# Four of the first key head's five projections, with their rotations, moved beside the last head of the full attention; the causal stage's later projections at other steps

## The chip, the cores and the metric

The kernel runs on one core of one Trainium2 chip. Its time is the device time of one launch, in microseconds (us): the median of three runs was 2612.7 us (2612.5 to 2613.82). TensorE (PE), VectorE (DVE), ScalarE (ACT) and GpSimd (POOL) run their own instruction streams in program order and meet at semaphores; SyncE (SP) issues the large transfers.

## The reference, cut to what matters

Two layers of a small model, each an attention-like part and a mixture of experts, on x of shape (2, 1024, 256). The change lies in the second layer: a full attention of three heads, a norm, and a causal attention with rotary embedding, 16 query heads in 4 groups that share a key head.

```python
# full attention, per batch b (0, 1) and head h (0, 1, 2)
scores = Q @ K.T / sqrt(256); w = softmax(scores over the queries' axis); attn = w @ V
x = x + ga * (mean(attn over the heads) @ fc_w.T + fc_b)
...
# causal attention, HD 128, per batch and key head (4), each with 4 query heads
q = x @ wq; k = x @ wk; v = x @ wv
apply_rope(x) = concat([x1 * cos - x2 * sin, x2 * cos + x1 * sin])
probs = softmax(causal(q @ k.T / sqrt(HD))); out = (probs @ v) @ wo
```

## The kernel before

The program is a chain of stages with a barrier between them: modulation, a state-space layer, the first experts, `attn1` (full attention), `attn2` (causal attention), the second experts. Every stage is written as a list `todo` that each engine's loop walks through in the same order, taking what is its own; so the list alone sets the order on each engine.

A float32 product is made of three passes: each operand is split into a high half (ACT copies it) and a low half (POOL or DVE subtracts), and PE multiplies high by high, high by low and low by high.

`attn1` has 2 batches x 3 heads x 8 rows of scores. One row: PE makes a score unit of 12 matmuls (L1545) into two banks of the accumulator memory; DVE takes the maximum (L1704); ACT makes the exponential (L1605) and its high half (L1610); POOL makes the low half (L1726); DVE makes the scaled values (L1682 to L1689); two rows later PE adds the row's `sum` of 24 matmuls (L1559). Score, key, value and flip (transpose) units share two pairs of banks in turn, so `unit_free` makes each unit wait until the unit two before it has been read: a score by the exponential, a key by its low half on DVE (L1701). DVE also does one piece of a list of `chores` after each row's maximum: in batch 1 those are the residual, the norm and the scaling for the causal stage. The two flips that make `hT` for `attn2` stand behind the last head's rows 6 and 7 and wait for the scaled rows (L1312).

`attn2` has 8 groups u (batch and key head), each with rows 7 to 0 of scores for four query heads. A group needs five projections (`project`, i = 0 the key, 1 to 4 the queries; PE L2143, 12 matmuls each). Each is rotated: DVE multiplies by cos and by sin from the accumulator (L1986 to L1988, called a rotation below), POOL adds the two products (`add`, L2009), ACT copies the high half (`high`, L2059), and the low half is subtracted on DVE for the key (L1992) and on POOL for the queries (`low`, L2014). Two pairs of buffers hold the products, so a query's rotation waits for the low half of the projection two before it:

```python
if i >= 3:
    dve.wait_ge(s["rope"], heads(u, i - 2))
elif i == 2:
    dve.wait_ge(s["rope_k"], u + 1)
```

For group 0 all five projections stand at the stage's start, followed by the four scores of row 7, the values unit and the first `turn`. For u > 0 they stand inside the previous group's rows 4 to 2, between `turn` (four transposes of the probabilities, L2178), `value` (L2188) and `out` (the row's output product, L2197). `turn` and `out` share two banks in turn (`ring_free`): a turn that comes two after an out waits until DVE has added that output to `hs` (L2002). While group 0 runs, DVE also works through 30 chores, one per turn (residual, statistics, norm).

Of the kernel before, what the change touches and what calls it, by code (L numbers as in the profile page):

```python
# [1328 lines left out]
class Ahead:  # L1329


    def __init__(self, ctx, nc, g, hs):
# [3 lines left out]
        self.hT, self.wh = ([sb(n + half, shape, F32R) for half in ("hi", "lo")] for n, shape in (("hT", [P, KC, L]), ("wh", [P, KC, WC])))  # L1336
        self.mask, self.ident_b = sb("mask", [P, P], BF16), sb("ident_b", [P, P], BF16)
# [35 lines left out]
def attn1(nc, g, pre, fc_w, fc_b, norm_w, wq, wk, wv):  # L1373
# [7 lines left out]
    with ctx:  # L1381
# [8 lines left out]
        wm = [sb("wm" + half, [P, 2 * AH, KC, D], F32R) for half in ("hi", "lo")]  # L1390
        late_hT = [sb("hT" + half, [P, KC, L], F32R) for half in ("hi", "lo")]
        fw, fbw = hs[:, TB:TB + KC, :], hs[:, TB + KC, :]
        kT = [sb("kT" + half, [P, 2, KC, L], F32R) for half in ("hi", "lo")]
# [11 lines left out]
        s_nb, s_e, s_eh, s_el, s_vs, s_av, s_acc = sem("nb"), sem("e"), sem("eh"), sem("el"), sem("vs"), sem("av"), sem("acc")  # L1405
        s_next, s_nh, s_nl, s_bf = sem("next"), sem("nh"), sem("nl"), sem("bf")
# [6 lines left out]
        def rows_of(b):  # L1413

            return hs[:, 0:TB, :] if b == 0 else hs[:, TB:2 * TB, :]

        PROJ = ("key", "key", "val", "val")

        def order():
# [34 lines left out]
        units = [t for t in todo if t[0] in ("flip", "key", "val", "score")]  # L1454
# [23 lines left out]
        def _(pe):  # L1478
# [16 lines left out]
            def unit_free(n):  # L1495

                if n >= 2:
                    t = units[n - 2]
                    if t[0] == "score":
                        pe.wait_ge(s_e, row[t[1:]] + 1)  # L1500
                    elif t[0] == "val":
                        pe.wait_ge(s_v, kept[t])
                    else:
                        pe.wait_ge(s_lo, split[t])

            for t in todo:
                what, b, h, i = t
                if what in ("flip", "key", "val", "score"):
# [3 lines left out]
                if what == "flip":  # L1512
# [4 lines left out]
                    tr.then_inc(s_unit, 1)  # L1517
                elif what == "key":
# [20 lines left out]
                elif what == "score":  # L1539
                    if i == 0:  # L1540
                        pe.wait_ge(s_lo, split["key", b, h, 1])
                    for c in range(2):
                        for k in range(KC):
                            for x_, y_ in THREE:
                                mm = pe.matmul(ps[:, o + c, :], kT[x_][:, (b * AH + h) % 2, k, i * P:(i + 1) * P], hT_of(b)[y_][:, k, c * 512:(c + 1) * 512],  # L1545
# [18 lines left out]
        def _(act):  # L1564
# [19 lines left out]
            roots = {(0, 0, 3): (1, 2), (1, 1, 1): (0, 3), (1, 2, 2): (0, 4)}  # L1584
            for t in todo:
# [4 lines left out]
                elif what == "key":  # L1590
                    act.wait_ge(s_unit, number[t] + 1)
                    act.activation(kT[HI][:, (b * AH + h) % 2, i, :], pair(number[t]), ACT.Copy).then_inc(s_hi, 1)
# [5 lines left out]
                elif what == "score":  # L1598
# [11 lines left out]
                    act.activation(eh[HI][:, r % RING, :], e[:, r % 2, :], ACT.Copy).then_inc(s_eh, 1)  # L1610
# [682 lines left out]
```

## Time and profile before

| what | us |
|---|---|
| median of three runs | 2612.7 |
| the profiled execution | 2608.71 |
| its span in the trace | 2606.8 |
| start of `attn1`'s first flip | 993.91 |
| end of `attn1` and start of `attn2` on PE | 1353.44 |
| first turn of `attn2` | 1410.43 |
| end of `attn2`, about | 2296.03 |

PE is busy for 2358.8 us, 90% of the span, DVE for 54%, ACT and POOL for 43% each. The profile is one execution. Its times are from the start of the span; "idle before" of a row names the engine and line that ended the wait. A matmul's busy time overlaps that of the next, so the pace is read from start to start.

### The profile page before, as it was taken

The numbers are of one execution on the slowest core, as the hardware profiler recorded it, in microseconds if no ns is written. First come the engines' busy times: TensorE is split into PE (matmuls) and PEld (weight loads), VectorE is DVE, ScalarE is ACT, GpSimd is POOL, SyncE is SP. The second block draws the span as 40 slices with busy tenths as digits, with TensorE's granted clock in tenths as the row PEclk, the third lists the DMA queues.
The fourth block names the chain that finished last, engine by engine and source line by source line (L and its number), as shares of the span: only waits on it lengthen the run. The fifth ranks groups of instructions, "written<-read, shape, count | busy, mean of one in ns | idle before, by whom it ended". The sixth has DMA issues, their size and how long they took to land. (4 is left out here: it accounts for less than half of the span.)

```text
span 2606.8 us, 34398 instructions
## 1 busy us (share of the span) xinstructions
PE 2358.8 (90%) x12718; PEld 1789.0 (69%) x12718; DVE 1400.7 (54%) x2467; ACT 1119.6 (43%) x1906; POOL 1125.9 (43%) x656
## 2 busy tenths in 40 slices
PE   6959999986999968999986999999999999949997
PEld 2339999964777746899974676777677677725554
DVE  6568888864222225545555855556455554463332
ACT  3467777721111114344433554545455454521121
POOL 0439999901332212443335455444545544203443
PEclk8979999997999988999998999999999999979999
DMA  6273271238211220000000000000000001045223
GB/s 242 94 306 69 75 306 70 102 101 271 49 31 32 34 77 32 1 1 1 1 21 33 21 1 21 21 1 21 1 21 3 18 9 33 1 151 160 44 44 63
DMA packets 109334, 168.33 MB, mean 65 GB/s; under 512 B 30546, under 2 KB 78674, under 8 KB 107092
## 3 DMA queue, kind: packets, MB, share of 16 engines
q1 hardware_dynamic: 94196, 145.35, 15.9%
q0 software_dynamic: 14976, 20.78, 4.8%
q8 instruction: 107, 1.75, 0.3%
q14 instruction: 55, 0.45, 0.1%
HBM read 115.94 MB, written 52.32 MB: 65 GB/s over the span
## 5 line engine op out<-in xcount | busy, mean ns | idle before, releaser
L638 POOL TENSOR_TENSOR mb_dbx<-mb_ud,mb_bb 128x1024 f32<-128x1024 f32 x128 | 302.0, 2364 | 56.2 <-DVE mb_h L496 40.7
L496 DVE TENSOR_TENSOR_SCAN mb_h<-ps,mb_dbx 128x1024 f32<-128x1024 f32 x128 | 292.2, 2288 | 47.9 <-ACT ps L608 37.4
L2025 POOL TENSOR_TENSOR a_e<-a_e,a_rc 128x1024 f32<-128x1024 f32 (+5 forms) x144 | 188.5, 1315 | 269.5 <-DVE a_rc L1945 269.2
L2188 PE MATMUL ps<-a_eT,a_v 128*128 128x512 f32 x576 | 297.4, 598 | 4.3 <-ACT a_eT L2069 4.3
L1955 DVE TENSOR_REDUCE a_mx<-ps 128x1 f32<-128x1024 f32 (+7 forms) x256 | 192.7, 753 | 196.1 <-PE ps L2167 195.4
L939 POOL DMA_INDIRECT e_acc<-e_hid,e_ids x78 | 123.7, 1586 | 370.8 <-DVE e_hid L1235 363.0
L2069 ACT ACTIVATE a_eT<-ps 128x512 f32<-128x512 f32 x288 | 171.1, 594 | 247.5 <-PE ps L2178 246.9
L740 PE MATMUL ps<-mb_dg,mb_hts 128*128 128x128 f32 x2048 | 250.7, 276 | 0.4
L740 PEld LDWEIGHTS ps<-mb_dg,mb_hts 128*128 128x128 f32 x2048 | 239.5, 192 | 1.9 <-issue 1.9
L2164 PE MATMUL ps<-a_kThi,a_qThi 128*128 128x512 f32 (+3 forms) x384 | 205.4, 535 | 22.7 <-DVE a_e L1988 11.0
L1221 DVE COPY e_work<-ps 128x256 f32<-128x256 f32 x78 | 33.2, 425 | 356.7 <-PE ps L1054 356.7
L1726 POOL TENSOR_TENSOR a_elo<-a_e,a_ehi 128x1024 fp32r<-128x1024 f32 x48 | 115.2, 2400 | 231.8 <-ACT a_ehi L1610 121.0
L2053 ACT ACTIVATE a_e<-ps,a_nb 128x1024 f32<-128x1024 f32 (+5 forms) x192 | 156.3, 814 | 91.9 <-DVE a_nb L1956 79.1
L1085 PE MATMUL ps<-e_wd,e_work 128*128 (+1 forms) x780 | 189.0, 384 | 1.9 <-ACT e_work L984 1.9
L1066 PE MATMUL ps<-e_wg,e_work 128*128 x468 | 178.2, 518 | 4.7 <-DVE e_work L1221 1.3
L978 ACT ACTIVATE e_hid<-ps 128x688 f32<-128x688 f32 (+1 forms) x78 | 52.5, 673 | 300.2 <-PE ps L1066 300.2
L617 ACT ACTIVATE mb_hts<-ps 128x512 f32<-128x512 f32 x256 | 139.2, 595 | 93.2 <-PE ps L725 93.2
L1066 PE MATMUL ps<-e_wu,e_work 128*128 x468 | 170.9, 501 | 0.0
L2178 PE MATMUL ps<-ident,a_e 128*128 128x128 f32 x992 | 150.3, 274 | 18.5 <-DVE hs L2002 16.2
L725 PE MATMUL ps<-ident,mb_h 128*128 128x128 f32 x1024 | 135.4, 276 | 32.6 <-DVE mb_h L496 32.4
L1085 PEld LDWEIGHTS ps<-e_wd,e_work 128*128 128x128 f32 (+1 forms) x780 | 138.9, 190 | 30.0 <-issue 15.8
L925 POOL DMA_INDIRECT e_xin<-e_rows,e_ids x78 | 77.2, 990 | 188.3 <-DVE e_ids L1210 164.5
(345 smaller groups left out, 5331.3 us busy)
## 6 DMA issues: line engine op xcount, KB each, us to landing
mb_bb<-mb_db_rows SPq DMA_DIRECT2D x16, 1024.0 KB, 12.2
mb_ddiag<-mb_dg SPq DMA_DIRECT2D x1, 8192.0 KB, 22.3
mb_dg<-mb_ddiag SPq DMA_DIRECT2D x8, 1024.0 KB, 13.3
e_wg<-in_g SPq DMA_DIRECT2D x8, 688.0 KB, 10.3
e_wu<-in_u SPq DMA_DIRECT2D x8, 688.0 KB, 10.5
e_wd<-in_d SPq DMA_DIRECT2D x8, 640.0 KB, 11.1
mb_dxa<-mb_bb SPq DMA_DIRECT2D x8, 512.0 KB, 2.6
mb_dz<-mb_xz SPq DMA_DIRECT2D x8, 512.0 KB, 2.9
```

Of the source, the lines that this page charges most:

```text
L496: dve.tensor_tensor_scan(h[:, at % 2, :], pair(at % 2), dbx[:, at % 2, :], 0.0, ALU.mult, ALU.add).then_inc(s_h, 1)
L638: pool.tensor_tensor(dbx[:, at % 2, :], ud[:, kk % 2, 0, :], bb[:, n, :], ALU.mult).then_inc(s_dbx, 1)
L740: mm = pe.matmul(ps[:, 6 + half, q * P:(q + 1) * P], hts[:, at % 2, c:c + P], dg[:, n, c:c + P], start=(n == 0 and q == 0), stop=(n == NS ...
L1066: mm = pe.matmul(ps[:, b0 + a, 0:FN], xT[:, i % 2, k * P:(k + 1) * P], w[:, ds(e), k, a * FN:(a + 1) * FN].rearrange("p a n -> p (a n)"), ...
L1085: mm = pe.matmul(ps[:, 6, 0:D], hT[0:n, i % 2, c * P:(c + 1) * P], wd[0:n, ds(e), c, :].rearrange("p a n -> p (a n)"), start=(c == 0), sto ...
L1955: own(dve.reduce_max(mx[:, q:q + 1], pair(n, (i + 1) * P), AX_X))
L2025: pool.tensor_tensor(probs(i, h), probs(i, h), rc[:, q:q + 1].to_broadcast([P, (i + 1) * P]), ALU.mult).then_inc(s["en"], 1)
L2053: act.activation(probs(i, h), pair(n, (i + 1) * P), ACT.Exp, bias=nb[:, q:q + 1], scale=SCALE, accum_out=sm[:, q:q + 1]).then_inc(s["e"], 1)
L2069: act.activation(eT[:, k % ER, :], ps[:, bank[what, u, i, h], :], ACT.Copy).then_inc(s["eT"], 1)
L2164: mm = pe.matmul(ps[:, o + t, 0:c1 - c0], qT[x_][:, j, i * P:(i + 1) * P], kT[y_][:, c0:c1], start=(x_ == y_), stop=(x_ == LO and not last))
L2178: tr = pe.transpose(ps[:, bank[token], h * P:(h + 1) * P], probs(i, h, j * P, (j + 1) * P), ident[:, :])
L2188: mm = pe.matmul(ps[:, 6 + rows[u, i] % 2, :], v[:, j, :], eT[:, k % ER, :], start=(j == 0), stop=(j == i))
```

## The change

Group 0's projections 0 to 3 (`AHEAD = 4`) go into `attn1`'s list as `rope` units, after rows 0, 2, 4 and 6 of the last head. Their rotations use one pair of product buffers (`turned`), so rotation i + 1 waits for the low half of projection i. To have `hT` ready, the two flips move one head earlier and DVE does two chores per row instead of one in batch 1 (the list got empty places so that the square roots on ACT still come in time). The results live in buffers that `attn1` no longer needs then. `attn2` starts with projection 4 alone. For u > 0 the projections stand at other turns, and the high halves follow one step later. The number of projections, rotations, adds, and halves is the same as before, except that the key's low half of group 0 is made on POOL instead of DVE.

```diff
+        AHEAD = pre.AHEAD
+        turned = [hs[:, TB + 4 * a:TB + 4 * a + 4, :].rearrange("p a d -> p (a d)") for a in range(2)]
...
-                        if h + 1 == AH and b + 1 == B and m >= 6:
+                        if (b, h) == (B - 1, AH - 2) and m >= 6:
                             todo.append(("flip", B, 0, m - 6))
+                        if (b, h) == (B - 1, AH - 1) and m % 2 == 0 and m // 2 < AHEAD:
+                            todo.append(("rope", B, 0, m // 2))
...
+                    elif t[0] == "rope":
+                        pe.wait_ge(s_rot, t[3] + 1)
...
+                elif what == "rope":
+                    if i == 0:
+                        pe.wait_ge(s_lo, split["flip", B, 0, 1])
+                        pe.wait_ge(s_nl, WPIECES)
+                    c0 = (REP if i == 0 else i - 1) * HD
+                    for c in range(2):
+                        for k in range(KC):
+                            for x_, y_ in THREE:
+                                mm = pe.matmul(ps[:, o + c, :], pre.wh[x_][:, k, c0:c0 + HD], pre.hT[y_][:, k, c * 512:(c + 1) * 512],
...
-            roots = {(0, 0, 3): (1, 2), (1, 1, 1): (0, 3), (1, 2, 2): (0, 4)}
+            roots = {(0, 0, 3): (1, 2), (1, 0, 5): (0, 3), (1, 1, 3): (0, 4)}
...
+                    if ropes:
+                        rope_high(ropes.pop(0))
...
-                    if chores[b]:
-                        chores[b].pop(0)()
+                    for _ in range(1 if b == 0 or (h, i) == (0, 0) else 2):
+                        if chores[b]:
+                            chores[b].pop(0)()
+                elif what == "rope":
+                    o, (a, c) = number[t], turned
+                    if i > 0:
+                        dve.wait_ge(s_roped, i)
+                    else:
+                        dve.wait_ge(s_hi, split["flip", B, 0, 1])
+                    dve.wait_ge(s_unit, o + 1)
+                    dve.tensor_tensor(a, pair(o), pre.cos, ALU.mult)
...
+                if what == "rope":
+                    pool.wait_ge(s_rot, i + 1)
+                    pool.tensor_tensor(turned[0], turned[0], turned[1], ALU.add).then_inc(s_turned, 1)
+                    ropes.append(i)
...
+                    if ropes:
+                        rope_low(ropes.pop(0))
...
-            ahead_proj = {(4, 0): 0, (4, 2): 1, (4, 4): 2, (3, 2): 3, (2, 1): 4}
-            for n in range(NPROJ):
+            ahead_proj = {(4, 0): 0, (4, 1): 1, (4, 3): 2, (3, 0): 3, (3, 3): 4}
+            for n in range(AHEAD, NPROJ):
                 put("project", 0, n, 0)
...
-                while unhigh and (unhigh[0][2] >= 3 or len(unhigh) > 2):
+                while unhigh and (unhigh[0][2] >= (3 if unhigh[0][0] == 0 else 4) or len(unhigh) > 2):
```

Three places in the built programs show what moved. First POOL at the end of `attn1` and the start of `attn2` (`a_elo` is a row's low half, `h_qklo` and `h_wmlo` are the low halves of the projections). Before, then after:

```order
L1726 TENSOR_TENSOR a_elo<-a_e,a_ehi 128x1024 x16
L1381 UNCONDITIONAL_BRANCH
L2004 UNCONDITIONAL_BRANCH
L2009 TENSOR_TENSOR a_e<-a_e 128x1024 x3
L2014 TENSOR_TENSOR a_qTlo<-a_e,a_qThi 128x1024
L2009 TENSOR_TENSOR a_e<-a_e 128x1024
L2014 TENSOR_TENSOR a_qTlo<-a_e,a_qThi 128x1024
L2009 TENSOR_TENSOR a_e<-a_e 128x1024
L2014 TENSOR_TENSOR a_qTlo<-a_e,a_qThi 128x1024 x2
```

```order
L1780 TENSOR_TENSOR hs<-hs 128x1024
L1787 TENSOR_TENSOR a_elo<-a_e,a_ehi 128x1024
L1774 TENSOR_TENSOR h_wmlo<-hs,h_wmhi 128x1024
L1787 TENSOR_TENSOR a_elo<-a_e,a_ehi 128x1024
L1780 TENSOR_TENSOR hs<-hs 128x1024
L1787 TENSOR_TENSOR a_elo<-a_e,a_ehi 128x1024
L1774 TENSOR_TENSOR h_wmlo<-hs,h_wmhi 128x1024
L1385 UNCONDITIONAL_BRANCH
L2069 UNCONDITIONAL_BRANCH
L2074 TENSOR_TENSOR a_e<-a_e 128x1024
L2079 TENSOR_TENSOR h_wmlo<-a_e,h_wmhi 128x1024
```

The adds and low halves now alternate with the rows' low halves in `attn1`, and one of each is left at the start of `attn2`.

Second PE near the output of row 4 (`a_wo`), in the rows before group 1 begins. The first transposes (`ident`) behind the output are free to go; the second ones wait for that output's add on DVE. Before, then after:

```order
L2143 MATMUL ps<-h_hThi,h_whlo 128x512
L2178 MATMUL ps<-ident,a_side 128x128 x4
L2197 MATMUL ps<-a_wo,a_ao 128x256 x4
L2188 MATMUL ps<-a_eT,a_v 128x512
L2178 MATMUL ps<-ident,a_side 128x128 x4
L2188 MATMUL ps<-a_eT,a_v 128x512
L2178 MATMUL ps<-ident,a_e 128x128 x4
```

```order
L2245 MATMUL ps<-ident,a_side 128x128 x4
L2264 MATMUL ps<-a_wo,a_ao 128x256 x4
L2255 MATMUL ps<-a_eT,a_v 128x512
L2208 MATMUL ps<-h_hThi,h_whhi 128x512
...
L2208 MATMUL ps<-h_hThi,h_whlo 128x512
L2245 MATMUL ps<-ident,a_side 128x128 x4
L2255 MATMUL ps<-a_eT,a_v 128x512
L2245 MATMUL ps<-ident,a_e 128x128 x4
```

Projection 3, which ended just ahead of the output's turn, now stands two turns earlier, and projection 4 comes between the output and the turn that waits for its add.

Third DVE while group 0's rows 4 and 3 run, from the end of one rotation (that of projection 2 before, of projection 3 after) over a chore of statistics (`n_st` to `n_var`) to the add of row 4's output (`hs<-ps,hs`). Before, then after:

```order
L1988 TENSOR_TENSOR x<-ps,raw 64x1024
L1269 BN_STATS n_st<-hs 128x6 x4
L1276 TENSOR_TENSOR n_mean<-n_st 128x8
...
L1285 TENSOR_SCALAR n_var<-n_var 128x8
L1986 TENSOR_TENSOR x<-ps,raw 128x1024
L1987 TENSOR_TENSOR x<-ps,raw 64x1024
L1988 TENSOR_TENSOR x<-ps,raw 64x1024
L2002 TENSOR_TENSOR hs<-ps,hs 128x256
```

```order
L2053 TENSOR_TENSOR x<-ps,raw 64x1024
L1269 BN_STATS n_st<-hs 128x6 x2
L1276 TENSOR_TENSOR n_mean<-n_st 128x8
...
L1285 TENSOR_SCALAR n_var<-n_var 128x8
L2067 TENSOR_TENSOR hs<-ps,hs 128x256
L2051 TENSOR_TENSOR x<-ps,raw 128x1024
```

The statistics stood ahead of the fourth rotation and now stand behind it, directly ahead of the output's add.

## Rows read from the trace of the kernel before

**Rows 1.** Busy time by stretch: us, then busy of PE, PEld, DVE, ACT, POOL, PEclk, DMA.

```profile
1353.40:1410.40 57.00, 33.00 (x143) 24.91 (x144) 27.48 (x32) 12.97 (x18) 27.90 (x12) 0.82 0.08 24
...
1472.20:1508.10 35.90, 31.54 (x143) 22.33 (x142) 34.79 (x42) 13.94 (x21) 15.78 (x6) 1.00 0.00 0
```

**Rows 2.** PE's waits, 1320 to 2296 us: us in total, times, longest.

```profile
PE ps L2178 <- DVE hs L2002: 16.2, 8, 3.5
PE ps L2164 <- DVE a_e L1988: 11.0, 2, 5.5
PE ps L2164 <- POOL a_qTlo L2014: 6.2, 1, 6.2
PE ps L1516 <- DVE hs L1312: 3.6, 1, 3.6
```

**Rows 3.** PE in order of time, start of the causal stage: start, us.

```profile
1353.44 0.47 PE L2143 MATMUL ps<-h_hThi,h_whhi 128*128 128x512 f32 x1 [0.32 <-PEq L1381]
...
1400.35 0.23 PE L2167 MATMUL ps<-h_mask,h_ident_b 128*128 128x128 bf16 x1
...
1410.43 0.63 PE L2178 MATMUL ps<-ident,a_e 128*128 128x128 f32 x4 [2.32 <-DVE a_e L1948]
```

**Rows 4.** DVE, POOL and ACT there, in order of time.

```profile
1382.40 1.23 DVE L1986 TENSOR_TENSOR a_e<-ps,raw 128x1024 f32<-128x1024 f32 x1 [4.85 <-POOL a_qTlo L2014]
...
1386.13 1.23 DVE L1955 TENSOR_REDUCE a_mx<-ps 128x1 f32<-128x1024 f32 x1
...
1377.63 2.37 POOL L2009 TENSOR_TENSOR a_e<-a_e 128x1024 f32<-128x1024 f32 x1 [3.88 <-DVE a_e L1988]
1379.95 2.35 POOL L2014 TENSOR_TENSOR a_qTlo<-a_e,a_qThi 128x1024 fp32r<-128x1024 f32 x1
...
1387.58 1.12 ACT L2053 ACTIVATE a_e<-ps,a_nb 128x1024 f32<-128x1024 f32 x1 [15.05 <-DVE a_nb L1956]
...
1391.80 1.99 ACT L2059 ACTIVATE a_qThi<-a_e 128x1024 fp32r<-128x1024 f32 x2
```

**Rows 5.** PE in the full attention's last head, in order of time.

```profile
1322.86 0.40 PE L1545 MATMUL ps<-a_hThi,a_kThi 128*128 128x512 f32 x1
...
1325.60 0.28 PE L1559 MATMUL ps<-a_vhi,a_ehi 128*128 128x256 f32 x1
...
1328.48 0.40 PE L1545 MATMUL ps<-a_hThi,a_kThi 128*128 128x512 f32 x1
```

**Rows 6.** POOL, DVE and PE where the first two keys are split.

```profile
1193.99 2.41 POOL L1726 TENSOR_TENSOR a_elo<-a_e,a_ehi 128x1024 fp32r<-128x1024 f32 x1 [5.27 <-PE ps L1559]
...
1258.49 2.39 POOL L1726 TENSOR_TENSOR a_elo<-a_e,a_ehi 128x1024 fp32r<-128x1024 f32 x1 [5.95 <-PE ps L1559]
...
1194.58 2.37 DVE L1654 TENSOR_TENSOR hs<-hs,mod 128x512 f32<-128x512 f32 x1 [4.06 <-ACT hs L1618]
...
1202.83 1.23 DVE L1701 TENSOR_TENSOR a_kTlo<-ps,a_kThi 128x1024 fp32r<-128x1024 f32 x1 [1.41 <-ACT a_kThi L1592]
...
1204.76 0.39 PE L1526 MATMUL ps<-a_hThi,a_wmhi 128*128 128x512 f32 x1
...
1260.92 0.39 PE L1526 MATMUL ps<-a_hThi,a_wmhi 128*128 128x512 f32 x1
```

**Rows 7.** PE and DVE near the fourth projection of head 2.

```profile
1606.66 0.60 PE L2178 MATMUL ps<-ident,a_side 128*128 128x128 f32 x4
1607.10 1.89 PE L2197 MATMUL ps<-a_wo,a_ao 128*128 128x256 f32 x8
1608.83 1.02 PE L2188 MATMUL ps<-a_eT,a_v 128*128 128x512 f32 x2
...
1613.12 0.63 PE L2178 MATMUL ps<-ident,a_e 128*128 128x128 f32 x4 [1.97 <-DVE hs L2002]
...
1608.82 1.22 DVE L1986 TENSOR_TENSOR x<-ps,raw 128x1024 f32<-128x1024 f32 x1 [4.93 <-POOL a_qTlo L2014]
```

**Rows 8.** DVE in the statistics of the norm, key head 0.

```profile
1492.22 2.32 DVE L1277 TENSOR_TENSOR n_t<-n_st 128x8 f32<-128x8 f32 x1
```

More of the change, by code:

```diff
@@ L1329 @@
 class Ahead:
+    AHEAD = 4
     def __init__(self, ctx, nc, g, hs):
@@ L1336, in __init__ @@
         self.hT, self.wh = ([sb(n + half, shape, F32R) for half in ("hi", "lo")] for n, shape in (("hT", [P, KC, L]), ("wh", [P, KC, WC])))
+        self.wm, self.qk = ([sb(n + half, [P, c, L], F32R) for half in ("hi", "lo")] for n, c in (("wm", REP - 1), ("qk", KC)))
+        self.kT = [q[:, 0, :] for q in self.qk]
+        self.qT = [[q[:, 1, :], *(w[:, h, :] for h in range(REP - 1))] for q, w in zip(self.qk, self.wm)]
         self.mask, self.ident_b = sb("mask", [P, P], BF16), sb("ident_b", [P, P], BF16)
@@ L1415, in rows_of, with roped @@
             return hs[:, 0:TB, :] if b == 0 else hs[:, TB:2 * TB, :]
+        AHEAD = pre.AHEAD
+        turned = [hs[:, TB + 4 * a:TB + 4 * a + 4, :].rearrange("p a d -> p (a d)") for a in range(2)]
+        def roped(i, half):
+            return pre.kT[half] if i == 0 else pre.qT[half][i - 1]
         PROJ = ("key", "key", "val", "val")
@@ L1453, in attn1 @@
         todo = order()
-        units = [t for t in todo if t[0] in ("flip", "key", "val", "score")]
+        units = [t for t in todo if t[0] in ("flip", "key", "val", "score", "rope")]
         number = {t: n for n, t in enumerate(units)}
@@ L1507, in _ @@
                 what, b, h, i = t
-                if what in ("flip", "key", "val", "score"):
+                if what in ("flip", "key", "val", "score", "rope"):
                     n = number[t]
@@ L1618, in _ @@
                         act.activation(flat(hs[:, 2 * q:2 * q + 2, :]), ps[:, 4 + q, :], ACT.Copy).then_inc(s_acc, 1)
+            for i in ropes:
+                rope_high(i)
         @block.vector
@@ L1758, in attn2 @@
         hT, wh = pre.hT, pre.wh
-        qT, kT = ([sb(n + half, shape, F32R) for half in ("hi", "lo")] for n, shape in (("qT", [P, REP, L]), ("kT", [P, L])))
+        qT, kT, AHEAD = pre.qT, pre.kT, pre.AHEAD
         v, eT = sb("v", [P, TB, HD]), sb("eT", [P, ER, REP * P])
@@ L2057, in high @@
                 a, _ = rotated(u)
-                act.wait_ge(s["sum"], u * NPROJ + i + 1)
-                act.activation(kT[HI][:, :] if i == KEY else qT[HI][:, i - 1, :], a[:, i % 2, :], ACT.Copy).then_inc(s["high"], 1)
+                act.wait_ge(s["sum"], u * NPROJ + i + 1 - AHEAD)
+                act.activation(kT[HI] if i == KEY else qT[HI][i - 1], a[:, i % 2, :], ACT.Copy).then_inc(s["high"], 1)
             for q in range(TB // 2):
```

76 lines of the change are left out of this document (48 added, 28 removed).

## The prediction

> **What bounds the kernel now.** I read the busy times by stretch first. PE is busy nearly throughout the two attention stages, so time is lost where PE stands still, and I looked for the stretches where it does. The largest is the start of the causal stage: 57.0 us pass between the first projection and the first turn, with PE busy for 33.0 of them at a mean granted clock of 0.82, which mixes the levels 2.4 and 1.2 GHz [rows 1, 3]. The list of PE's waits says who ends them: 11.0 us in two waits for a rotation on DVE, 6.2 us for a low half on POOL [rows 2]. The order of time shows why. A rotation takes 3.7 us on DVE (from 1382.40 to the maximum at 1386.13), POOL's add 2.37 and low half 2.35, and the next rotation but one may only start when that low half is done [rows 4]. So projections that cost PE 2.7 us each go by at 8.5 us each, and nothing else is there to do. The same list shows the other two waits that this change touches: 3.6 us, once, of the first flip for the scaled rows, and 16.2 us in eight turns that wait for the add of an output on DVE [rows 2]. Six of the eight are alike, one per group from 1 to 6, 1.97 us each [rows 7]; the other two lie in group 0 and are the remaining 4.4 us. The end of the program hangs on PE through these stages; what PE gains here, the second experts begin earlier.
>
> **Term 1, the full attention's last head.** Four projections come in. A score unit has the same 12 matmuls and takes 2.74 us (1322.86 to 1325.60), so four cost 11.0 us of PE [rows 5]. The flips only move, and their wait of 3.6 us should go: the scaled rows are now made in the middle head's row 5, a row ahead of the first flip. A row's pace is 5.62 us [rows 5], two rows and a projection 14.0. In these DVE does two maxima with their values, some 5 us, and one rotation of 3.7. POOL does two low halves of rows (2.4 each, rows 6), one add and one low half, 9.5 in all. Both fit. The tightest link is that rotation i + 1 waits for low half i, behind the next row's low half on POOL: counted from the end of score m, the rotation ends at 6.5, the add at 10.4, POOL's next row low at about 14.5 and the projection's low half at 16.9, while PE delivers the next projection at 16.7. The rotation then has until about 25 us before a later unit wants its banks. So I cost the rotations at nothing. Their cover is 3.7 us deep: beyond that, PE pays.
>
> The chores at double pace are not free. In batch 1, row 1 now has two residual pieces and row 2 two more; they stand ahead of the low half of the next head's first key, and the next key on PE (1204.76) waits for that low half, which before was ready at 1204.06, 0.7 us ahead [rows 6]. The pieces added ahead of it are 2.8 us when DVE has its way. One of them can meet POOL's low half: the row at 1194.58 shows such a product taking 2.37 us, ending just after POOL's operation that began at 1193.99 for 2.41 us [rows 6]. I work out a stall of 0.8 us if DVE gets through and 3.0 us if it waits once, and take the middle, 1.9. The Trainium skill (SBUF — State Buffer, section Who interferes with whom) says that a DVE instruction with two SBUF inputs and a GpSimd instruction that reads SBUF lock each other out for a whole instruction, whoever starts first. By that rule DVE's piece could as well hold POOL off, which is the 0.8 end; by the row it is the 3.0 end. The second place is row 2 of the middle head: eight statistics and the small operations stand together ahead of the same kind of low half, while POOL runs from 1258.49 for 2.39 us and PE wants the key at 1260.92 [rows 6]. Small operations of this kind do get held: 2.32 us instead of 0.17 for one of 128x8 [rows 8]. That gives 2.4 us if held, 0 if not; the row is near, so 2.4. Term 1 is 11.0 - 3.6 + 1.9 + 2.4 = 11.7 us lost.
>
> **Term 2, the causal stage's start.** From its first matmul: projection 4 ends at 2.7, its rotation at 6.4. Score 0 ends at 4.2 (six matmuls, half of a full-attention score, and the mask). Score 1 wants the projection's banks: 6.4 to 7.9. Score 2 wants score 0's banks: maximum to 7.7, exponential 1.1 with 0.2 to read its sum, so 9.2 to 10.7. On ACT the high half of query 4 stands behind the second exponential, which ends at 10.6; it ends at 11.7 (1.99 for two, rows 4), POOL's low half at 14.1. Score 3 waits for that: 14.1 to 15.6 at 2.4 GHz, to 17 at 1.2, as the clock falls in such gaps; I take 16.3. From the end of that score to the first turn the work is unchanged: 1400.58 to 1410.43, 9.8 us [rows 3]. The turn comes at 26.1 instead of 57.0: 30.9 us won, with bounds of 29 and 32. POOL's scaling of the probabilities starts behind the low half at 14.1, three of 1.9, and is done by 20, before the turn needs it.
>
> **Term 3, groups 1 to 6.** A turn two steps behind row 4's output waits for its add, and the add stands behind the fourth rotation, which began only at 1608.82, released by a low half on POOL; hence 1.97 us at 1613.12 [rows 7]. DVE's and POOL's order is unchanged here; PE's is not. Projections 1, 2 and 3 come one to two turns earlier, and projection 4, 2.74 us, now lies between the output and the waiting turn. Counted from the end of projection 0, with 0.44 for a turn, 1.73 for an output (1606.66, 1607.10, 1608.83), some 0.9 for a value product and 2.74 for a projection, PE reaches that turn at 26.1. DVE: rotation 1 ends at 7.8, the key's low half at 9.0, rotation 2 at 14.9; POOL's add and low half at 19.6; rotation 3 at 23.4, the add at 23.8. So 2.3 us to spare, and the whole wait goes: 6 x 1.97 = 11.8 us. ACT's high half of query 4 now stands ahead of the next turn's copy and ends at 35.3, while the copy is needed at 37.2: hidden, 1.9 us deep. The wait for the exponential one step on stays.
>
> **Term 4, group 0.** DVE is full there: 34.8 of 35.9 us busy [rows 1]. The add of row 4's output now has the chore of statistics directly ahead of it, and that runs when POOL does its add and low half (4.7 us). Counted from the first rotation: rotation 2 ends at 17.0, POOL's low half at 21.8, rotation 3 at 25.5; POOL holds the small operations until 30.2; they end at 31.9 and the add at 32.3. PE arrives at 27.1. From there it needs 5.3 us to the first score (8.0 before, less a projection), 37.6 against 35.9, and the norm's last chore, also behind a rotation, costs about 0.8 more. So 2.5 us lost, with bounds of 3 won (chores not held) and 5 lost.
>
> **Sum.** 11.7 - 30.9 - 11.8 + 2.5 = -28.5 us. Against the profiled execution, 2608.71, this is 2580.2; the median of the runs is 4.0 us above that execution, so 2584.2, and I say 2584.
>
> **Rivals.** First, all waits go: DVE gets through at both places of term 1 (0.8 instead of 4.3) and all 16.2 us of the turns go. Then 11.0 - 3.6 + 0.8 - 30.9 - 16.2 = -38.9, or 2574. For it: PE has the slack in time; against it: the held operations in rows 6 and 8. Second, the turns' waits only move: another output or the late high half on ACT takes the 1.97 us per group. Then 11.8 is missing: 2596. For it: the rotations' own chain is no shorter; against it: a cover of 2.3 us. Third, the last head pays in part: if each of the three later rotations slips beyond its 3.7 us by 3, PE loses 9 and the time is 2593. Fourth, slower than before: in the last head the chain is not covered at all, because DVE, waiting for low half i, keeps the next row's maximum and so the exponential behind it. Then each of four steps costs the chain of 8.5 us, 34 us in all, and the time is 2618. It decides from 7.2 us of stall per step on, where the 28.5 are used up. Against it: low half i is due at 16.9, within 0.2 of the projection it would be waiting for anyway. That the change does nothing is no case: the 57 us stretch cannot keep its five rotations when one is left.
>
> **How the numbers follow.** A measurement of this kernel tells 0.2%, 5.2 us, from no change. I give the forecast 0.58, the first rival 0.14, the second 0.16, the third 0.09, the fourth 0.03. The range from 2572 to 2597 holds the first three and its own bounds (2578 to 2591). Faster by over 0.2%: 0.96; within 0.2%: 0.02; slower: 0.02.
>
> **What would show it.** In the profile of the changed kernel: the start of the causal stage to its first turn takes about 26 us; no wait of the first flip; four rotations in the last head, each released by PE and not by POOL; two waits of keys for low halves on DVE of 1 to 3 us; in groups 1 to 6 no turn waits for an output's add, and one in group 0 waits for about 5 us. The prediction is wrong if PE stands still between rows of the last head, or if the turns' waits stay at 2 us.

## The result and the profile after

The changed kernel takes 2582.32 us (median of four runs, 2579.41 to 2586.73), the kernel before 2613.26 us beside it: a ratio of 0.9879, interval 0.9867 to 0.9892, 30.9 us less. The forecast was 2584 us, and its range (2572 to 2597) held the time. The profiled execution of the changed kernel happens to be the longest of its four runs, 2586.73 us with a span of 2584.8. It is 22.0 us below the profiled execution of before. The other 9 us lie in which executions were profiled: that of before was 4.6 us under its median, that of the changed kernel is 4.4 over its own. The part on term 2 shows one stretch that differs by as much from one execution to another; where the 4.6 us lie isn't shown.

Busy time by stretch, as in [rows 1]: the causal stage from its first projection to its first turn, then on to group 1's first score behind an exponential.

```profile
1367.55:1401.59 34.04, 24.99 (x96) 20.78 (x96) 11.61 (x19) 8.72 (x14) 10.29 (x5) 0.65 0.14 39
1401.59:1511.91 110.32, 97.89 (x464) 67.93 (x464) 93.06 (x181) 55.63 (x112) 51.78 (x33) 0.97 0.10 32
```

PE's waits from 1190 to 2296 us, as in [rows 2]:

```profile
...
PE ps L2245 <- DVE hs L2067: 5.9, 2, 4.9
PE ps L2231 <- ACT a_e L2118: 5.3, 8, 1.8
PE ps L2231 <- POOL h_wmlo L2079: 4.4, 1, 4.4
...
PE ps L1554 <- DVE h_qklo L1741: 2.8, 1, 2.8
PE ps L2231 <- DVE a_e L2053: 2.4, 1, 2.4
PE ps L2245 <- DVE a_e L2013: 2.3, 1, 2.3
PE ps L1554 <- DVE a_kTlo L1741: 2.0, 1, 2.0
```

The first line shown stands against 16.2 us in eight waits [rows 2]: the six of 1.97 us in groups 1 to 6 are gone, two in group 0 are left. The first flip's 3.6 us are gone. The 11.0 and 6.2 us of the start have become 2.4 and 4.4. New are two stalls at keys, 2.8 and 2.0 us.

The differences of the two profiled executions, from the same marks on PE in both:

| stretch | before | after | difference |
|---|---|---|---|
| first flip of `attn1` to start of `attn2` | 359.53 | 373.34 | +13.8 |
| start of `attn2` to its first turn | 56.99 | 34.04 | -22.95 |
| to group 1's waiting score (1516.05, 1511.91) | 105.62 | 110.32 | +4.7 |
| to group 7's (2193.83, 2171.64) | 677.78 | 659.73 | -18.05 |
| all else | | | +0.5 |
| span | 2606.8 | 2584.8 | -22.0 |

### The profile page after: what moved, and what is told of

The parts are those of the page before. It is cut to its first block and busy times, and to the rows that moved or that the text cites. A ratio compares the mean times of both kernels' runs of the same rounds, so it can differ in the third digit from the quotient of the medians.

```text
span 2584.8 us, 34395 instructions
## 1 busy us (share of the span) xinstructions
PE 2360.9 (91%) x12718; PEld 1794.3 (69%) x12718; DVE 1411.2 (55%) x2466; ACT 1118.6 (43%) x1906; POOL 1128.4 (44%) x657
## 5 line engine op out<-in xcount | busy, mean ns | idle before, releaser
L2231 PE MATMUL ps<-h_qkhi,h_wmhi 128*128 128x512 f32 (+3 forms) x288 | 153.2, 532 | 12.0 <-ACT a_e L2118 5.3
```

Of the source, the lines that this page charges most:

```text
L2231: mm = pe.matmul(ps[:, o + t, 0:c1 - c0], qT[x_][j][:, i * P:(i + 1) * P], kT[y_][:, c0:c1], start=(x_ == y_), stop=(x_ == LO and not last))
```

## The experiments

Each kernel was timed against the kernel before on the same chip. "Less than the changed kernel" compares the medians, 2582.32 for the changed one; the kernel before took 2611.95 to 2614.60 us beside them, so a difference of under 3 us between two of these medians tells nothing by itself, and the stretches of the profiles must decide.

### The two parts alone

The kernel before with the projections of groups 1 to 7 at their new turns:

```diff
-            ahead_proj = {(4, 0): 0, (4, 2): 1, (4, 4): 2, (3, 2): 3, (2, 1): 4}
+            ahead_proj = {(4, 0): 0, (4, 1): 1, (4, 3): 2, (3, 0): 3, (3, 3): 4}
...
-                while unhigh and (unhigh[0][2] >= 3 or len(unhigh) > 2):
+                while unhigh and (unhigh[0][2] >= (3 if unhigh[0][0] == 0 else 4) or len(unhigh) > 2):
```

> The kernel before with the later projections at their new turns and the late high half, all five projections of key head 0 still in the causal stage. If the two parts of the change add up: the six waits of 1.97 us of a turn for an output's add go, groups 1 to 6 are 18 us shorter in the profile (11.8 of waits, 6 of TensorE at half clock behind three of them), group 0 is 3 us longer: 15 us less than before. Rival, that the turns' waits went because the heads part freed DVE or POOL: the waits stay near 2 us and the time is within 3 us of before. Rival on the clock, that only the waits go and the 6 us are chance of one profile: 9 us less.

Measured 2596.03 us, ratio 0.9933 (0.9921 to 0.9946), 15.9 us less than before (2611.95 on that chip). This is what was expected (15 us), and both rivals are out. Groups 1 to 6 take 659.7 us as in the changed kernel, group 0 from its first turn to group 1's values unit 118.4 against 113.9.

The second is the changed kernel with the same two lines turned back:

> The changed kernel with the later projections back at their old turns: only the four projections beside the last head. If the parts add up: start of the causal stage to its first turn 34 us as in the changed kernel, last head 13.8 us longer than before, six waits of 1.97 us back in groups 1 to 6: 9 us less than before, with group 0's cold start perhaps 8. Rival, that the two parts need each other (the late positions free POOL in group 0, which then delays the start): no gain, or under 4 us.

Measured 2595.57 us, ratio 0.9930 (0.9918 to 0.9942), 16.4 us less than before. The two parts together give 32.3 us, the change gives 30.9: they add up, and neither needs the other. But 9 us were expected of this one. Its six waits in groups 1 to 6 are back, as expected; what was not expected lies in a stretch where the two programs hold the same instructions, the start of the causal stage. By stretch, and PE in order of time:

```profile
1366.47:1391.92 25.45, 16.32 (x95) 13.24 (x96) 11.61 (x19) 8.84 (x14) 10.28 (x5) 1.00 0.18 53
```

```profile
1381.19 0.47 PE L2231 MATMUL ps<-h_qkhi,h_wmhi 128*128 128x512 f32 x1 [3.50 <-POOL h_wmlo L2079]
...
1382.68 0.30 PE L2216 MATMUL ps<-h_whhi,h_hThi 128*128 128x128 f32 x1
...
1391.92 0.63 PE L2245 MATMUL ps<-ident,a_e 128*128 128x128 f32 x4 [2.32 <-DVE a_e L2013]
```

The same rows of the changed kernel:

```profile
1383.51 0.77 PE L2231 MATMUL ps<-h_qkhi,h_wmhi 128*128 128x512 f32 x1 [4.37 <-POOL h_wmlo L2079]
...
1386.31 0.46 PE L2216 MATMUL ps<-h_whhi,h_hThi 128*128 128x128 f32 x1
...
1396.59 0.73 PE L2231 MATMUL ps<-h_qkhi 128*128 128x512 f32 x1
...
1401.59 1.09 PE L2245 MATMUL ps<-ident,a_e 128*128 128x128 f32 x4 [2.32 <-DVE a_e L2013]
```

The values unit that follows score 3 takes 10.3 us in the changed kernel's profile (1386.31 to 1396.59) and 5.4 here (1382.68 to 1388.07, the start of the score behind it); the stretch as a whole runs at 2.4 GHz here (granted clock 1.00) and at a mean of 0.65 there, 34.04 us against 25.45.

### The chores of the full attention

One chore entry per row again, in batch 1, with some entries holding two pieces; none of the added pieces stands ahead of a first key's low half:

```diff
-                      1: [lambda: None, *[lambda q=q: residual(q) for q in range(4)], *[lambda q=q: norm.stats(x, 4 * q, 4) for q in range(2)],
+                      1: [lambda: None, lambda: residual(0), lambda: residual(1), lambda: residual(2),
+                          lambda: (residual(3), norm.stats(x, 0, 4)), lambda: (norm.stats(x, 4, 4), norm.spread(0, False)), lambda: None,
...
+                          lambda: (norm.stats(hs, 0, TB), norm.spread(0, True)), lambda: None,
+                          lambda: (norm.inverse(0, 4), scaled(0), scaled(1), small())]}
...
-                    for _ in range(1 if b == 0 or (h, i) == (0, 0) else 2):
-                        if chores[b]:
-                            chores[b].pop(0)()
+                    if chores[b]:
+                        chores[b].pop(0)()
```

> The changed kernel with the full attention's batch 1 chores spread anew: one residual piece per row in rows 1 to 3, the second statistics at row 3 of the middle head and not at row 2, so that no added piece stands ahead of the low half of a first key. If the two stalls of PE at keys (2.77 and 2.02 us) come from those pieces, and the half clock behind each (about 1 us each) from the stalls, both go: 5 to 7 us less than the changed kernel. Rival, that the stalls come from the row's own work on DVE held by POOL: they stay or move to the next key and the gain is under 2 us. The new lump of three operations at row 5 could cost 1 to 2 us at the flips.

Measured 2580.05 us (2573.21 to 2581.06), ratio 0.9862 (0.9846 to 0.9878), 2.3 us less than the changed kernel by the medians. Both stalls are gone from the list of PE's waits, and what came is one of 0.5 us at the first flip. `attn1` takes 363.8 us instead of 373.3 in its profile, of which 1.7 lie in batch 0, where nothing differs; 7.8 is therefore the chores' part. Three later kernels that hold the same edit have 365.4, 365.5 and 363.8, so that figure is steadier than the median, over which the start of the causal stage lays its own spread (33.5 us here). In the changed kernel, DVE and POOL at the first key, then at the second, and PE at the first:

```profile
1203.21 2.75 DVE L1695 TENSOR_TENSOR x<-x,hs 128x512 f32<-128x512 f32 x1
1205.99 1.23 DVE L1741 TENSOR_TENSOR h_qklo<-ps,h_qkhi 128x1024 fp32r<-128x1024 f32 x1
...
1202.55 2.86 POOL L1787 TENSOR_TENSOR a_elo<-a_e,a_ehi 128x1024 fp32r<-128x1024 f32 x1 [6.59 <-ACT a_ehi L1644]
...
1262.69 2.40 DVE L1279 TENSOR_TENSOR n_var<-n_st 128x8 f32<-128x8 f32 x1
...
1262.67 2.39 POOL L1787 TENSOR_TENSOR a_elo<-a_e,a_ehi 128x1024 fp32r<-128x1024 f32 x1 [4.88 <-PE ps L1587]
```

```profile
1207.27 0.79 PE L1554 MATMUL ps<-a_hThi,h_wmhi 128*128 128x512 f32 x1 [2.77 <-DVE h_qklo L1741]
1207.87 0.63 PE L1554 MATMUL ps<-a_hTlo,h_wmhi 128*128 128x512 f32 x1
1208.29 0.63 PE L1554 MATMUL ps<-a_hThi,h_wmlo 128*128 128x512 f32 x1
```

The second residual's product, 0.69 us when POOL is still, takes 2.75; one small operation of 0.17 takes 2.40. Behind the stall PE's matmuls start 0.43 us apart and not 0.23, the pace of 1.2 GHz. The two stalls are 4.8 us. From score unit to score unit across each key the changed kernel is 4.6 and 3.9 us longer than before, 8.5 us in all: the other 3.7 us are the clock behind the stalls. The new order of chores gives 0.7 of the 8.5 back at the flips, hence 7.8.

### Group 0

The chores of group 0 at double pace from turn 11 on, so that the last one stands at row 4's first turn:

```diff
-                    c += [lambda: norm.spread(1, True), lambda: None, lambda: (norm.inverse(1, 2), dve.sem_inc(s["spare"], 1))]
-                    assert len(c) <= BLOCKS
+                    c += [lambda: norm.spread(1, True), lambda: None, lambda: None, lambda: None, lambda: (norm.inverse(1, 2), dve.sem_inc(s["spare"], 1))]
...
-                    if extra:
-                        extra.pop(0)()
+                    for _ in range(2 if u == 0 and turned[u, i, h] > 10 else 1):
+                        if extra:
+                            extra.pop(0)()
...
-                    if turns in (10, 29):
+                    if turns in (10, 21):
...
```

> The changed kernel with group 0's chores at double pace from turn 11 on, so that all but one are done before row 4. If the chores ahead of the outputs' adds cause the waits of 1.03 and 4.87 us, both go and group 0 is 6 to 7 us shorter: 6 us less than the changed kernel. Rival, that the add waits for the rotations (chain through POOL) and the chores only fill DVE's waits: the 4.87 stays, and rows 6 and 5, where DVE now has two chores per turn, get waits of their own: 0 to 3 us more.

Measured 2578.95 us (2575.67 to 2581.98), ratio 0.9867 (0.9852 to 0.9882), 3.4 us less. Both waits for an add are gone, but group 0 is only 2.1 us shorter (116.5 us against 118.6). And 1.5 of the 2.1 us lie ahead of the edit, between the first turn and the first value products, where the two kernels hold the same instructions (13.3 us against 14.8) and only the clock differs: granted clock 1.00 in the first five microseconds against 0.64. The edit itself is worth 0.6 us. Three rows of PE hold what came in place of the two waits:

```profile
1434.03 1.35 PE L2255 MATMUL ps<-a_eT,a_v 128*128 128x512 f32 x2 [2.43 <-ACT a_eT L2134]
...
1464.41 0.47 PE L2208 MATMUL ps<-h_hThi,h_whhi 128*128 128x512 f32 x1 [2.08 <-ACT a_e L2118]
...
1493.35 1.13 PE L2255 MATMUL ps<-a_eT,a_v 128*128 128x512 f32 x2 [0.53 <-ACT a_eT L2134]
```

For the first, two chores of centring stand together ahead of a maximum (3.48 us on DVE), and ACT has nothing to do for 2.99 us and then does the exponential ahead of the turn's copy:

```profile
1428.89 3.48 DVE L1301 TENSOR_SCALAR hs<-x,n_mean,n_rstd 128x256 f32<-128x256 f32 x4
1432.29 0.41 DVE L2019 TENSOR_REDUCE a_mx<-ps 128x1 f32<-128x256 f32 x1
```

So a second edit moves only the small operations at the list's end (spread, root, inverse) into group 1's row 7:

```diff
-                    c += [lambda: norm.spread(1, True), lambda: None, lambda: (norm.inverse(1, 2), dve.sem_inc(s["spare"], 1))]
                     assert len(c) <= BLOCKS
+                elif u == 1:
+                    c += [lambda: None, lambda: None, lambda: norm.spread(1, True), lambda: None, lambda: None, lambda: None,
+                          lambda: (norm.inverse(1, 2), dve.sem_inc(s["spare"], 1))]
...
-                    if turns in (10, 29):
+                    if turns in (10, 41):
...
```

> The changed kernel with the last chores of group 0 (the small operations of the norm, the root on ACT, the inverse) moved into group 1's row 7, where no output's add is near. If the second turn's wait for an add (4.87 us, and TensorE at half clock for some 5 us behind it) comes from the small operations that POOL holds, it goes and nothing new comes up: group 0 from its first turn to group 1's values unit 118.5 us becomes 112 to 113: 5 to 6.5 us less than the changed kernel. Rival, that rotation 3 itself is late: 3 us or more of the wait stay, 1 to 3 us less. Group 1 stays at 109.5 if DVE has the room there.

Measured 2579.45 us, ratio 0.9876 (0.9859 to 0.9893), with runs from 2574.25 to 2586.16 us, too wide for its median to tell 3 us. The profile tells: group 0 takes 109.9 us instead of 118.6, 8.7 less, and group 1 110.7 instead of 109.5. The same 1.5 us of clock behind the first turn are in the 8.7, so the edit is worth 7.2 us less 1.2, 6.0 us. The wait of 4.87 us is gone altogether, so rotation 3 itself was not late; the wait of 1.03 us at the earlier turn stays. By stretch from the first turn to the waiting score, beside the 110.32 us and 93.06 us of DVE above:

```profile
1397.47:1499.07 101.60, 94.70 (x464) 65.76 (x464) 81.06 (x167) 52.76 (x109) 50.32 (x33) 1.00 0.11 34
```

Fourteen small operations of DVE are gone from it and 12.0 us of DVE's busy time with them. What they did in the changed kernel, on DVE and POOL:

```profile
1490.46 0.75 DVE L1269 BATCH_NORM_STATS2 n_st<-hs 128x6 f32<-128x256 f32 x2
1491.25 1.64 DVE L1276 TENSOR_TENSOR n_mean<-n_st 128x8 f32<-128x8 f32 x1
1492.93 2.26 DVE L1277 TENSOR_TENSOR n_t<-n_st 128x8 f32<-128x8 f32 x1
...
1496.52 0.42 DVE L2067 TENSOR_TENSOR hs<-ps,hs 128x256 f32<-128x256 f32 x1
...
1500.81 2.19 DVE L1293 TENSOR_TENSOR n_t<-n_var,n_rstd 128x8 f32<-128x8 f32 x1
1503.03 2.34 DVE L1294 TENSOR_TENSOR n_t<-n_t,n_rstd 128x8 f32<-128x8 f32 x1
1505.40 2.34 DVE L1295 TENSOR_SCALAR n_t<-n_t 128x8 f32<-128x8 f32 x1
...
1490.51 2.35 POOL L2074 TENSOR_TENSOR x<-x 128x1024 f32<-128x1024 f32 x1 [3.88 <-DVE x L2053]
1492.82 2.34 POOL L2079 TENSOR_TENSOR h_wmlo<-x,h_wmhi 128x1024 fp32r<-128x1024 f32 x1
```

### The start of the causal stage

The changed kernel with group 0's values unit ahead of its fourth score:

```diff
             for h in range(REP):
+                if h == 3:
+                    put("values", 0, 0, 0)
                 put("score", 0, 7, h)
             for u in range(U):
-                put("values", u, 0, 0)
+                if u > 0:
+                    put("values", u, 0, 0)
```

> The changed kernel with the values unit of group 0 ahead of the fourth score of row 7 instead of behind it. It fills the 4.4 us in which PE waits for the low half of query 4. Filling the wait alone: 4.4 us less. If besides the values unit then runs at 2.4 GHz (5.4 us instead of 10.3): 9 to 11 us less, first turn 22 to 25 us after the stage's start instead of 34. Rival: the clock has already fallen in the two short waits before it, so the unit takes 10 us again, the score behind it too: 4 us less.

Measured 2575.13 us (2574.34 to 2576.53), ratio 0.9857 (0.9842 to 0.9872), 7.2 us less, with the first turn 23.8 us after the start.

With the values unit directly behind projection 4, and the high half of query 4 one place earlier for it:

```diff
+            put("values", 0, 0, 0)
             for h in range(REP):
                 put("score", 0, 7, h)
...
+                while unhigh and (unhigh[0][2] >= (1 if unhigh[0][:2] == [0, REP] else 3 if unhigh[0][0] == 0 else 4) or len(unhigh) > 2):
```

> The changed kernel with the values unit of group 0 directly behind projection 4, ahead of all scores, and the high half of query 4 ahead of the first exponential on ACT. PE then has 11 us of work before anything waits. If the loss at the start is the half clock that the waits bring: the values unit takes 5.4 us at 2.4 GHz and the first turn comes 19.5 to 21 us after the start: 13 to 14 us less than the changed kernel. Rival: the clock falls in the scores' waits that remain (scores 2 and 3, and 3.5 us ahead of the first turn), so that the first turns run at half clock: 8 to 10 us less.

Measured 2577.78 us (2573.47 to 2578.49), ratio 0.9868 (0.9853 to 0.9883), 4.5 us less. Its profile is its shortest run, 8.8 us under the changed kernel's median; by stretch:

```profile
1367.50:1388.40 20.90, 16.16 (x95) 13.14 (x95) 11.57 (x19) 8.83 (x14) 10.39 (x5) 0.99 0.22 64
```

The start is as expected, 13.1 us under the changed kernel's profile; against the 25.45 us that the old order takes when its clock holds, it is 4.5. By the median the gain is smaller than both expectations. In its profile the granted clock is 0.70 in the five microseconds behind the first turn, as the rival had it; what the runs that weren't profiled did there is not shown.

With nothing but the high half of query 4 ahead of the second exponential on ACT:

```diff
-                while unhigh and (unhigh[0][2] >= (3 if unhigh[0][0] == 0 else 4) or len(unhigh) > 2):
+                while unhigh and (unhigh[0][2] >= (2 if unhigh[0][:2] == [0, REP] else 3 if unhigh[0][0] == 0 else 4) or len(unhigh) > 2):
```

> The changed kernel with the high half of query 4 ahead of the second exponential on ACT instead of behind it, where ACT stands still for 1.8 us; nothing else moves. If the start is the chain rotation, add, high half, low half, score 3, that score starts 12.8 us after the stage's start and not 16: 3 us less, and as the wait of 4.4 us of PE shrinks to 1.2, the half clock should come less often: up to 8 us less. Rival, that score 3 waits for the exponential of score 1 (banks) as well: it ends at 12.5, so nothing is left of this rival if 12.8 shows; if 14 or more shows, POOL or the banks decide.

Measured 2575.15 us (2573.93 to 2577.29), ratio 0.9849 (0.9834 to 0.9864), 7.2 us less. Score 3 starts 12.95 us after the stage (1368.17), the first turn 23.7:

```profile
1381.12 0.47 PE L2231 MATMUL ps<-h_qkhi,h_wmhi 128*128 128x512 f32 x1 [1.37 <-POOL h_wmlo L2079]
```

So the chain of term 2 holds here to 0.15 us (12.8 expected, 12.95 measured), and by the medians one operation one place earlier is worth as much as the larger moves. Part of the 10 us by which the start is shorter than in the changed kernel's profile is the clock, 0.93 here against 0.65.

### The cover in the last head

The four projections after rows 0, 1, 2 and 3 instead of 0, 2, 4 and 6:

```diff
-                        if (b, h) == (B - 1, AH - 1) and m % 2 == 0 and m // 2 < AHEAD:
-                            todo.append(("rope", B, 0, m // 2))
+                        if (b, h) == (B - 1, AH - 1) and m < AHEAD:
+                            todo.append(("rope", B, 0, m))
```

> The changed kernel with the four projections of the last head after rows 0, 1, 2 and 3 instead of 0, 2, 4 and 6. The forecast's cover of 3.7 us was for two rows (14.0 us) against a chain of 10.4 to 14.5 us plus DVE's rows. With one row between (8.4 us) the chain of rotation, add, row low, low half decides: DVE stands for low half i and keeps the next maximum behind it, each of three steps costs 3 to 6 us: 10 to 17 us more than the changed kernel. Rival: the chain is shorter than worked out and PE is not held: within 2 us of the changed kernel.

Measured 2603.12 us (2600.32 to 2608.42, 11 runs), ratio 0.9967 (0.9957 to 0.9976), 20.8 us more than the changed kernel. POOL, DVE and PE there:

```profile
1331.42 2.37 POOL L1780 TENSOR_TENSOR hs<-hs 128x1024 f32<-128x1024 f32 x1 [3.81 <-DVE hs L1761]
1340.16 2.39 POOL L1787 TENSOR_TENSOR a_elo<-a_e,a_ehi 128x1024 fp32r<-128x1024 f32 x1 [6.37 <-PE ps L1587]
1342.51 2.34 POOL L1774 TENSOR_TENSOR h_qklo<-hs,h_qkhi 128x1024 fp32r<-128x1024 f32 x1
...
1344.88 1.23 DVE L1759 TENSOR_TENSOR hs<-ps,raw 128x1024 f32<-128x1024 f32 x1 [10.42 <-POOL h_qklo L1774]
...
1348.63 0.80 PE L1543 MATMUL ps<-h_hThi,h_whhi 128*128 128x512 f32 x1 [5.88 <-DVE hs L1761]
```

A step is 17.23 us (1331.40 to 1348.63) and not the 8.3 of a row and a projection, 8.9 more. This is the mechanism of the fourth rival, DVE standing for the low half and holding the row's maximum behind it, in two of the four steps at about its price of 8.5 us; in all it costs 21 us and not 34. PE's three stalls there are 5.88, 5.88 and 3.07 us, within the expected 10 to 17; from the score ahead of the second projection to the end of the stage 21.8 us are lost, and the 7 us beyond the stalls are matmuls at 1.2 GHz behind them: the projection at 1331.40 takes 5.3 us instead of 2.7. The expectation had left that out. In the changed kernel, with two rows per projection, it does not happen; DVE at the third rotation, POOL's low half ahead of it, and the projection on PE:

```profile
1338.60 0.48 DVE L1729 SCALAR_TENSOR_TENSOR a_vlo<-a_v,a_rc,a_vhi 128x256 fp32r<-128x256 f32 x1
1339.01 1.21 DVE L1759 TENSOR_TENSOR hs<-ps,raw 128x1024 f32<-128x1024 f32 x1
...
1336.03 2.38 POOL L1774 TENSOR_TENSOR h_qklo<-hs,h_qkhi 128x1024 fp32r<-128x1024 f32 x1
...
1335.27 0.39 PE L1543 MATMUL ps<-h_hThi,h_whhi 128*128 128x512 f32 x1
```

The low half ends at 1338.41, the values of the row keep DVE until 1339.01, so the low half costs nothing, with 0.6 us to spare on DVE, and PE doesn't stand still between these rows.

### The edits together

Chores, double pace in group 0 and values unit behind projection 4:

> The changed kernel with the three edits together: chores spread anew in the full attention, group 0's chores early, values unit directly behind projection 4. If they add up: 5 to 7, 6, and 13 us, 24 to 26 us less than the changed kernel, 2557. Rival: they share time (the cold clock of the start reaches into group 0, DVE is full earlier when the first turn comes earlier): 15 to 20 us less.

Measured 2565.42 us (2563.61 to 2567.82), ratio 0.9821 (0.9808 to 0.9835), 16.9 us less than the changed kernel: the rival's size. In its profile `attn1` takes 365.4 us and the start 20.95, as in the single edits; what is missing lies in group 0, which takes 117.8 us against the changed kernel's 118.6.

With the small operations moved to group 1 in place of the double pace, and the values unit behind projection 4, then in the gap:

> The changed kernel with the full attention's chores spread anew, the small operations in group 1, and the values unit of group 0 directly behind projection 4. If the gains add up: last head and chores 8 (measured), group 0 6, start of the causal stage 4.5 to 13: 19 to 25 us less than the changed kernel, 2558 to 2563, and 2 to 6 less than the kernel with the chores early. Rival: with the stalls gone elsewhere group 0's first score waits for ACT as before and the small operations only move their wait into group 1: within 2 us of that kernel.

> As the last one, but with the values unit in the gap ahead of the fourth score. By the profiles of the two orders alone (20.9 and 23.8 us to the first turn) it is 3 us slower than the last one; by the medians of the runs (2577.8 and 2575.1) it is 2 to 3 us faster. Whichever holds tells whether the short start keeps its clock in most runs.

The first measured 2559.31 us (2555.36 to 2562.31), ratio 0.9787 (0.9774 to 0.9800), 23.0 us less than the changed kernel and the fastest kernel here. It is as expected, and most of the 6 us that it gains over the kernel with the chores early lie in group 0 (111.0 us against 117.8, less 1.2 in group 1). The second measured 2567.18 us (2558.14 to 2570.87), ratio 0.9817 (0.9801 to 0.9834). Here the order of the profiles holds and not that of the earlier medians (20.9 against 23.3 us to the first turn), but the medians are 7.9 us apart and not 3. The second's 13 us of spread goes with mean clocks of its runs from 0.958 to 0.963. What makes it spread stays open: the same order without the other edits spread over 2.2 us only.

## Why the prediction was right, point by point

**Term 1, 11.7 forecast, 13.8 in the profile.** The mechanism was right: four projections at 2.7 us each of extra pace (8.34 us from score to score instead of 5.62), the flip's wait gone, no rotation waited for. The chores were forecast at 1.9 + 2.4 us of stalls; the stalls are 2.8 and 2.0, and the row that was put forward for the held operation (2.37 us, 2.75 measured) was the right one: POOL's operation had begun first, at 1202.55, and DVE's product at 1203.21 was held. What failed is the size, in which the clock was left out on both sides. From score to score the four projections are 10.9 us, the two keys 8.5 (4.8 of stalls, 3.7 of half clock), the moved flips -4.8 (the wait of 3.6 and 1.2 of half clock behind it), and 0.7 us less lie in batch 0, where nothing differs.

**Term 2, 30.9 won forecast, 23.0 in the profile, 31.5 when the clock holds.** The step "score 3, 14.1 to 15.6 at 2.4 GHz, to 17 at 1.2" let the clock cost something in one score and took "the work is unchanged, 9.8 us" from there to the first turn. In the changed kernel's profile scores 1 and 2 were already in part at half clock, so that score 3 began at 15.96 us and not at 14.1 (14.72 where the clock held). And the 9.8 us of before hold a values unit at granted clock 1.00; in the changed kernel's profile that unit ran at half clock, 10.3 us instead of 5.4. In the two-parts experiment everything ran at full clock, and the start took 25.45 us, 0.65 from the forecast. The sign that the forecast gave for itself, about 26 us to the first turn, did not show in the changed kernel's profile. Over six profiles that hold the same instructions there, the start took:

| kernel | start to first turn, us | granted clock |
|---|---|---|
| changed kernel | 34.04 | 0.65 |
| chores | 33.50 | 0.69 |
| group 0's chores early | 28.86 | 0.82 |
| small operations late | 28.86 | 0.82 |
| projections close together | 27.24 | 0.81 |
| first key head alone | 25.45 | 1.00 |

So the term was no single number: with short waits of 2.3 to 4.4 us in this stretch the clock falls in five of the six profiles, for longer or shorter, and in one not at all, and 8.6 us hang on it, about the spread of the changed kernel's runs (7.3). The forecast's bounds of 29 and 32 us won were too narrow on one side. The Trainium skill (TensorE: Matmul & The Clock Gate, Part 1) says that the gate watches activity in windows that run freely and do not begin anew with the kernel, so that where the clock changes varies between runs of one kernel. The six rows are compatible with that rule. No run here was made to move the stretch against such a window, so the cause of the differences stays argued.

One reading of the prediction is off, though no term hangs on it: it is not the projections that went by at 8.5 us each, but the last rotations (1373.85 to 1382.40). The five projections of before had all started 15.6 us into the stage (1369.01).

**Term 3, 11.8 won forecast, 18.05 measured.** All six waits went, as the count from projection 0 had it, and the second rival (the waits only move) is out: the late high half of query 4 costs nothing in any group. The sizing failed the same way as in term 1. By stretch, groups 1, 3 and 5 of before:

```profile
1524.30:1636.00 111.70, 109.21 (x566) 80.20 (x565) 59.88 (x129) 58.03 (x118) 53.82 (x36) 1.00 0.04 12
...
1747.70:1863.80 116.10, 113.52 (x582) 82.69 (x581) 67.70 (x139) 59.74 (x120) 54.14 (x36) 0.99 0.04 12
...
1975.50:2088.80 113.30, 110.80 (x566) 81.18 (x565) 59.85 (x129) 58.01 (x118) 53.75 (x36) 0.98 0.04 12
```

Three of the six groups give 2.2 us (111.7 to 109.5); the other three had fallen to half clock behind their wait and give 3.8 (113.3 to 109.5, and 116.1 to 112.3 in the group with the flips). Which groups fall is not fixed by the program: in the kernel with the old turns, which has the same six waits, five of the six are of the longer kind, and its groups 1 to 6 take 681.05 us against 677.78.

**Term 4, 2.5 lost forecast, 4.7 measured.** The two turns that wait for an add, before and then after:

```profile
1485.48 0.66 PE L2178 MATMUL ps<-ident,a_e 128*128 128x128 f32 x4 [0.88 <-DVE hs L2002]
1500.17 0.63 PE L2178 MATMUL ps<-ident,a_e 128*128 128x128 f32 x4 [3.48 <-DVE hs L2002]
...
1478.29 0.66 PE L2245 MATMUL ps<-ident,a_e 128*128 128x128 f32 x4 [1.03 <-DVE hs L2067]
1497.09 0.87 PE L2245 MATMUL ps<-ident,a_e 128*128 128x128 f32 x4 [4.87 <-DVE hs L2067]
```

The wait for row 4's add was forecast at 5.2 us (32.3 less 27.1) and is 4.87; the small operations that POOL holds are its cause, as moving them showed. The two waits together grew by 1.5 us, which is less than the 2.5 forecast for them and the last chore. The other 3.2 us are clock. Half of it is from the first turn to the first value products, 14.8 us against 13.3, which is the end of the start's half clock. The other half is behind the second wait: 14.8 us to the next group's score, against 13.1 for the same work before (15.9 less a projection). The kernel with the old turns bears this out: its two waits are those of before (0.87 and 3.48 us), and its group 0 is still 2.0 us longer, with granted clock 0.66 in the five microseconds after its first turn and 0.68 behind its 3.48 us wait.

**The sum.** All four terms left out the clock behind waits: it made term 3 a larger gain and the others smaller gains or larger losses. Against the profile the errors are +2.1, +7.9, -6.2 and +2.2, +6.0 us together, and 0.5 us lie elsewhere: for the profiled execution the forecast is 2580.2 us, and it took 2586.73. The median, 2582.32 us, is only 1.7 us from the forecast because the two profiled executions lie on opposite sides of their medians. So the good agreement is in part luck. Of the rivals, the first is out (5.9 us of the turns' waits and both stalls at keys stayed), and so is the third (PE doesn't stand still between the rows of the last head).

## What to carry to other kernels

Price a wait of a few microseconds on TensorE as the wait plus what runs at half clock behind it: here 1.97 us waits were worth 2.2 or 3.8 us, and two stalls of 4.8 us in all 8.5. Small vector operations are not small beside GpSimd: fourteen of them cost DVE 12.0 us; put them where no one waits for what is queued behind them, and don't bunch them. A chain over four engines that shares one pair of product buffers needs room between its steps, and how much is worth working out: with two rows between the projections it caused no wait, with one it cost 20.8 us.

## What the runs showed of the hardware that was not expected

The same 96 matmuls of the start, in the same order, took 25.45 to 34.04 us in six profiles, with mean granted clocks from 1.00 to 0.65. A TENSOR_SCALAR of 128x8 with one tensor input was held by POOL as long as operations with two (2.34 us, at 1505.40), while the statistics of 128x256 beside the same work took 0.75 us for two, and a rotation's product out of the accumulator memory (1326.78, 1.22 us) kept its pace beside a POOL operation that began at 1327.21. POOL is stretched too when DVE was first: the operation at 1202.55, begun beside a residual's first product, took 2.86 us instead of 2.39, and the product queued behind took the 2.75.
